# A graph layer on one core: 128 of a bucket's gathered rows are fetched row by row from the SyncE and ScalarE queues

## The reference

```python
h = maximum(layernorm(x), 0)
semb = h[src] @ tokeys.T
oemb = h[src] @ toqueries.T
values = exp(sum(semb * relations[rel] * oemb, axis=1) / 128)
fr = src + n * rel
values = values / segment_sum(values, fr)[fr]
output = segment_sum(values[:, None] * h[dst], fr).reshape(16, n, 128)
weights = einsum('rb,bij->rij', comps, bases_w)
out = x + relu(einsum('rij,rnj->ni', weights, output))
```

## Time and profile before

| | |
|---|---|
| median of 3 runs | 2524.19 us (2522.42 to 2524.29) |
| the profiled execution's own time | 2523.76 us |
| its span, from the first to the last instruction | 2522.1 us |
| POOL busy | 1699.4 us, 67% of the span |
| DVE busy | 1449.6 us, 57% |
| PE busy | 1407.6 us, 56% |
| ACT busy | 506.2 us, 20% |
| DMA engines busy from 510 to 2522 us | 21% |

### The profile page before, as it was taken

The page is one execution under the profiler, slowest core; times in us unless marked ns, Lnnn a source line. Parts: engine busy times, 40 slices in busy tenths (PEclk is TensorE's granted clock), DMA queues, the critical chain, the costliest instruction groups (busy, mean ns, idle before and its releaser), DMA issues.

```text
span 2522.1 us, 30851 instructions
## 1 busy us (share of the span) xinstructions
PE 1407.6 (56%) x9509; PEld 1047.1 (42%) x9510; DVE 1449.6 (57%) x2495; ACT 506.2 (20%) x968; POOL 1699.4 (67%) x1825
## 2 busy tenths in 40 slices
PE   4999999844445454544545364544545364544543
PEld 3666666623424243333424243333434243443423
DVE  7999999965454545445454544445454545445450
ACT  4666666511010101111110101111110101111110
POOL 3333344367777777777777777777777777777775
PEclk9999999966766676766666666766666666766666
DMA  5222222212222222222222222222222222222222
GB/s 156 120 119 115 112 114 119 100 46 55 56 53 56 53 56 53 56 53 56 55 54 55 54 55 54 55 53 56 55 54 55 54 55 54 55 54 55 54 55 41
DMA packets 76390, 169.04 MB, mean 67 GB/s; under 512 B 29162, under 2 KB 43730, under 8 KB 69943
## 3 DMA queue, kind: packets, MB, share of 16 engines
q0 software_dynamic: 52576, 105.77, 16.4%
q1 hardware_dynamic: 23442, 62.88, 6.6%
q10 hardware_dynamic: 352, 0.14, 0.0%
HBM read 112.09 MB, written 56.57 MB: 67 GB/s over the span
## 4 chain that ended last, share of the span: by engine, by line
POOL 58%; issue 20%; PE 17%; DMA 1%; DVE 1%; POOLq 1%; ACT 1%; SPq 0%; DVEq 0%; ACTq 0%
POOL arena L432 58%; PE bank L1055 7%; PE bank L1040 3%; PE bank L1011 1%; PE bank L1013 1%; ACT PFS L875 1%; POOLq L424 1%; DMA bucket_streams<-REC,IDXW 1%; PE bank L1019 1%; PE bank L1016 1%; PE bank L1015 1%; PE bank L1047 1%; DMA stage<-in_edge_type 0%; PE bank L1048 0%; PE bank L1158 0%
## 5 line engine op out<-in xcount | busy, mean ns | idle before, releaser
L432 POOL DMA_INDIRECT arena<-Z_messages,IDX x1593 | 1504.3, 944 | 490.7 <-issue 485.2
L1158 PE MATMUL bank<-arena 128*128 128x128 f32 x3528 | 510.6, 318 | 759.2 <-DMA arena<-Z_messages,IDX 759.2
L1158 PEld LDWEIGHTS bank<-arena 128*128 128x128 f32 x3528 | 502.7, 233 | 769.0 <-issue 769.0
L714 DVE SCALAR_TENSOR_TENSOR O<-bank,X 128x128 f32<-128x128 f32 x49 | 14.3, 292 | 734.1 <-PE bank L1158 734.1
L955 ACT COPY pay_all<-bank 128x1024 bf16<-128x1024 bf16 x147 | 108.0, 807 | 1368.1 <-PE bank L1125 1339.2
L395 POOL DMA_INDIRECT bucket_streams<-REC,IDXW x50 | 87.9, 1758 | 270.8 <-ACT REC L895 135.0
L706 DVE TENSOR_TENSOR arena<-stage,bank 128x512 f32<-128x512 bf16 x441 | 267.9, 682 | 0.3 <-PE bank L1146 0.2
L649 DVE TENSOR_TENSOR stage<-bank,NLF 128x4608 bf16<-128x4608 f32 x49 | 242.4, 4948 | 0.0
L1115 PE MATMUL bank<-stage,OHR 128*128 128x512 bf16 (+1 forms) x441 | 196.4, 611 | 50.7 <-DVE arena L706 44.4
L1146 PE MATMUL bank<-pay_all 128*128 128x256 bf16 x882 | 135.4, 282 | 114.7 <-DVE arena L706 110.0
L1055 PE MATMUL bank<-WT,HT 128*128 128x512 f32 x392 | 183.9, 609 | 0.0
(11 more groups left out here) (168 smaller groups left out, 1819.3 us busy)
## 6 DMA issues: line engine op xcount, KB each, us to landing
Z_messages<-stage SPq DMA_DIRECT2D x48, 1024.0 KB, 3.9
arena<-Z_messages,IDX POOLq DMA_INDIRECT x1593
X<-in_x SPq DMA_DIRECT2D x4, 768.0 KB, 12.8
out<-O SPq DMA_DIRECT2D x48, 64.0 KB
arena<-in_L_gnn_bases_w SPq DMA_DIRECT2D x1, 1024.0 KB, 15.0
bucket_streams<-arena SPq DMA_DIRECT2D x1, 882.0 KB
RL<-bucket_streams SPq DMA_DIRECT2D x49, 18.0 KB
Z_messages<-stage SPq DMA_DIRECT2D x1, 848.0 KB
```

The costliest lines, as they stand in the source:

```text
L432: g.indirect_dma_start(Gbuf[par][:, k, :], None, Z, bass.IndirectOffsetOnAxis(IDX[par][:, k:k + 1], 0))\
L1158: mm = t_.matmul(bank[2][:, 0:EMB], OW[:, k, :], Gbuf[par][:, k, :], start=(k == 0), stop=(k == G - 1))
```

## The change

The first of a bucket's tiles, which POOL gathered, is now fetched row by row. SP fetches its rows 0 to 63 and ACT its rows 64 to 127. Each row is a DMA of its own of 512 bytes. Its row number in `Z` comes from a register, and eight such registers are filled by one load from SBUF. POOL gathers tiles 1 and up. The 36 products of the sum stay.

DVE makes the row numbers of the first tile in one partition (`FIRST`), by a copy and a shift ahead of the `IDX` shift. PE's sum waits for one semaphore more (`row`). The count of POOL's gathers that PE waits for is lower by one in each bucket. SP and ACT wait at the start of the second stage until the table `Z` is stored.

```diff
+def first_tile(b, par):            # on SP; rows 0 to 63
+    sp.wait_ge(s["idx"], b + 1)
+    sp.sem_inc(s["sp_go"], 1)
+    if dyn(b) or b >= 2:
+        sp.wait_ge(s["acc"], b - 1)
+    sp.sem_inc(s["sp_go"], 1)
+    for p in range(0, P // 2, 8):
+        _, rows = nc.values_load_multi_w_load_instructions(
+            FIRST[par][:, 1, p:p + 8], engines=[mybir.EngineType.SP], ...)
+        for k in range(8):
+            sp.dma_start(Gbuf[par][p + k:p + k + 1, 0, :], Z[bass.ds(rows[k], 1), :]).then_inc(row[par], 16)
 def bucket(b, par):                # SP
-    if dyn(b) or b < NB:
-        if dyn(b) or b >= 2:
-            sp.wait_ge(s["rl_t"], b - 1)
-        sp.dma_start(RL[par][:, :], stream[bass.ds(b * (STRIDE // P), G), :]).then_inc(rl[par], 16)
+    if dyn(b) or b + 1 < NB:
+        load_records(b + 1, 1 - par)
+    first_tile(b, par)
     if dyn(b) or b >= 2:
         store_out(b - 2, par)
...
-                    for k in range(FLOOR):           # POOL, gather
+                    for k in range(1, FLOOR):
                         tile(k)
...
                 def gather_index(b, par):          # DVE
+                    v.tensor_copy(FIRST[par][:, 0, :], RL[par][0:1, :]).then_inc(s["first"], 1)
+                    dve.wait_ge(s["first"], b * 2 + 1)
+                    v.tensor_scalar(FIRST[par][:, 1, :], FIRST[par][:, 0, :], 7, None, ALU.logical_shift_right)\
+                        .then_inc(s["first"], 1)
+                    dve.wait_ge(s["first"], b * 2 + 2)
                     v.tensor_scalar(IDX[par][:], RI[:], 7, None, ALU.logical_shift_right).then_inc(s["idx"], 1)
...
                     if dyn(b) or b + 1 < NB:       # ACT, bucket
                         spread_relations(b + 1, 1 - par)
+                    first_tile(b, par)             # as on SP, rows 64 to 127
...
                     pe.wait_ge(gat[par], g_total)  # PE, aggregate
+                    pe.wait_ge(row[par], row_total)
```

More of the change, by code:

```diff
@@ L161, in program @@
         zrow = sb("zrow", [2 * R, EMB], F32)
-        NT = sb("NT", [NB, 6], F32)
+        NT = sb("NT", [NB, 7], F32)
         NTI = sb("NTI", [NB, 2], I32)
@@ L170, in program @@
         IDX = [sb(f"IDX{p}", [P, G], I32) for p in range(2)]
+        FIRST = [sb(f"FIRST{p}", [1, 2, P], I32) for p in range(2)]
         NLI = sb("NLI", [P, 2, G], I32)
@@ L198, in program @@
             h th ht so_mm so_sb prod z_mm z_sb zst0 zst1 zrow v nt nt_mm nt_row marks_sb marks_st
-            rl0 rl1 rl_t ri dec nlf idx inv rrf ohn ohr ord vr cnt cm cx cs masks x3 w w3 bd tp oht lk ow gat0 gat1 acc o ost0 ost1
+            rl0 rl1 rl_t ri dec nlf idx inv rrf ohn ohr ord vr cnt cm cx cs masks x3 w w3 bd tp oht lk ow gat0 gat1 row0 row1 sp_go act_go first acc o ost0 ost1
             pool_go pe_go iota_p
@@ L207, in program @@
         ost = [s["ost0"], s["ost1"]]
+        row = [s["row0"], s["row1"]]
         x_in = [s[f"x_in{k}"] for k in range(5)]
@@ L292, in _, with load_records @@
             with sp.If(bad < 1):
+                def load_records(b, par):
+                    if dyn(b) or b >= 2:
+                        sp.wait_ge(s["rl_t"], b - 1)
+                    sp.dma_start(RL[par][:, :], stream[bass.ds(b * (STRIDE // P), G), :]).then_inc(rl[par], 16)
+                def first_tile(b, par):
+                    sp.wait_ge(s["idx"], b + 1)
+                    sp.sem_inc(s["sp_go"], 1)
+                    if dyn(b) or b >= 2:
+                        sp.wait_ge(s["acc"], b - 1)
+                    sp.sem_inc(s["sp_go"], 1)
+                    for p in range(0, P // 2, 8):
+                        _, rows = nc.values_load_multi_w_load_instructions(
+                            FIRST[par][:, 1, p:p + 8], engines=[mybir.EngineType.SP], min_val=0, max_val=ZROWS - 1,
+                            skip_runtime_bounds_check_because="a record holds a row of Z or the empty row")
+                        for k in range(8):
+                            sp.dma_start(Gbuf[par][p + k:p + k + 1, 0, :], Z[bass.ds(rows[k], 1), :]).then_inc(row[par], 16)
                 def bucket(b, par):
-                    if dyn(b) or b < NB:
-                        if dyn(b) or b >= 2:
-                            sp.wait_ge(s["rl_t"], b - 1)
-                        sp.dma_start(RL[par][:, :], stream[bass.ds(b * (STRIDE // P), G), :]).then_inc(rl[par], 16)
+                    if dyn(b) or b + 1 < NB:
+                        load_records(b + 1, 1 - par)
+                    first_tile(b, par)
                     if dyn(b) or b >= 2:
@@ L305, in store_out @@
                     sp.dma_start(out[bass.ds(b * P, n), :], O[par][0:n, :]).then_inc(ost[par], 16)
+                sp.wait_ge(zst[0], 16 * ((NB + 1) // 2))
+                sp.wait_ge(zst[1], 16 * (NB // 2))
+                load_records(0, 0)
                 bucket(0, 0)
@@ L603, in _ @@
             chain(v.tensor_scalar(NT[:, 1:2], NTI[:, 1:2], float(FLOOR), None, ALU.max), "nt")
+            chain(v.tensor_scalar(NT[:, 6:7], NT[:, 1:2], 1.0, None, ALU.subtract), "nt")
             chain(v.tensor_scalar(PARI[:, 1:2], PARI[:, 0:1], 1, None, ALU.bitwise_and), "nt")
-            chain(v.tensor_tensor(NT[:, 3:4], NT[:, 1:2], PARI[:, 1:2], ALU.mult), "nt")
-            chain(v.tensor_tensor(NT[:, 2:3], NT[:, 1:2], NT[:, 3:4], ALU.subtract), "nt")
+            chain(v.tensor_tensor(NT[:, 3:4], NT[:, 6:7], PARI[:, 1:2], ALU.mult), "nt")
+            chain(v.tensor_tensor(NT[:, 2:3], NT[:, 6:7], NT[:, 3:4], ALU.subtract), "nt")
             chain(v.tensor_scalar(NT[:, 4:5], MX[:], float(WIN), None, ALU.is_gt), "nt")
@@ L958, in bucket, with first_tile @@
                         spread_relations(b + 1, 1 - par)
+                    first_tile(b, par)
+                def first_tile(b, par):
+                    act.wait_ge(s["idx"], b + 1)
+                    act.sem_inc(s["act_go"], 1)
+                    if dyn(b) or b >= 2:
+                        act.wait_ge(s["acc"], b - 1)
+                    act.sem_inc(s["act_go"], 1)
+                    for p in range(P // 2, P, 8):
+                        _, rows = nc.values_load_multi_w_load_instructions(
+                            FIRST[par][:, 1, p:p + 8], engines=[mybir.EngineType.Activation], min_val=0, max_val=ZROWS - 1,
+                            skip_runtime_bounds_check_because="a record holds a row of Z or the empty row")
+                        for k in range(8):
+                            a.dma_start(Gbuf[par][p + k:p + k + 1, 0, :], Z[bass.ds(rows[k], 1), :]).then_inc(row[par], 16)
+                act.wait_ge(zst[0], 16 * ((NB + 1) // 2))
+                act.wait_ge(zst[1], 16 * (NB // 2))
                 spread_relations(0, 0)
@@ L1086, in _ @@
             pe.wait_ge(s["v"], NCH)
-            pe.wait_ge(s["nt"], 10)
+            pe.wait_ge(s["nt"], 11)
             t_.matmul(bank[3][0:1, 0:NB], NT[:, 1:2], identf[0:NB, 0:NB], start=True, stop=True)
@@ L1149, in lookups, with aggregate @@
                         mm.then_inc(s["lk"], 1)
-                def aggregate(b, par):
-                    g_total = pe.value_load(ROWI[0:1, bass.ds(b + (1 + par) * NB, 1)], min_val=16 * FLOOR, max_val=16 * G * (NB + 1) // 2)
+                def aggregate(b, par, row_total):
+                    g_total = pe.value_load(ROWI[0:1, bass.ds(b + (1 + par) * NB, 1)], min_val=16 * FLOOR - 16, max_val=16 * G * (NB + 1) // 2)
                     pe.wait_ge(s["ow"], b * 9 + 9)
                     pe.wait_ge(gat[par], g_total)
+                    pe.wait_ge(row[par], row_total)
                     if dyn(b) or b >= 1:
@@ L1160, in aggregate, with stepb @@
                     mm.then_inc(s["acc"], 1)
-                def stepb(b, par, rl_total):
+                def stepb(b, par, rl_total, row_total=0):
                     if dyn(b) or b + 1 < NB:
@@ L1168, in stepb @@
                     if dyn(b) or b >= 1:
-                        aggregate(b - 1, 1 - par)
+                        aggregate(b - 1, 1 - par, row_total)
                     if dyn(b) or b < NB:
@@ L1174, in _ @@
                 stepb(0, 0, 16)
-                stepb(1, 1, 32)
+                ROWS = 16 * P
+                stepb(1, 1, 32, ROWS)
                 with pe.Fori(1, (NB - 1) // 2) as j:
[L1177 to L1180, removed]
+                    stepb(j * 2, 0, j * 16 + 16, j * ROWS)
+                    stepb(j * 2 + 1, 1, j * 16 + 32, j * ROWS + ROWS)
+                stepb(NB - 1, 0, 0, (NB - 1) // 2 * ROWS)
+                stepb(NB, 1, 0, (NB + 1) // 2 * ROWS)
             with pe.If(bad > 0):
```

## The result

| | before | changed |
|---|---|---|
| median | 2523.61 us (2522.42 to 2524.29, 4 runs) | 2463.59 us (2462.7 to 2464.11, 4 runs) |
| the profiled execution, its span | 2523.76, 2522.1 us | 2462.7, 2461.0 us |

The ratio is 0.9762 with a 95% interval of 0.9745 to 0.9779. The kernel is 60 us faster. The forecast was 2653 us and slower; what happened is its Rival 1 (2463 us): POOL stays the bound.

The account below looks back on a forecast made before the run. The prediction took POOL's gather issue as the present bound and ACT's row fetching, 42.9 us per bucket, as the new one. 533.9 + 49 x 42.9 + 15.4 + 1.7 = 2653 us, 5% slower; range 2458 to 2900 us.

Parts of the forecast that it names:

- Rival 1: Second stage: POOL stays the bound and all row work on SP and ACT is hidden, 2463 us; chance 0.34.
- POOL's part: POOL's gathers: 49 of 1593 go, saving 61.2 us; 39.4 us per bucket, 2462.6 us if POOL remains slowest.
- the price of ACT's bucket: ACT's queue: 64 row transfers, 8 loads and 0.5 us for the rest take 42.9 us per bucket, slowest of all.
- c: Step from one row transfer to the next on a queue: 0.46 us on SP, 0.50 on ACT.
- L: One load of eight registers on SP or ACT: 1.3 us, the middle between 0.3 and 2.3.
- The range: Whole kernel's time: 2458 to 2900 us, leaving out the far end of 3579 us.
- SP's 41.2 us: SP's queue per bucket: 64 x 0.46 + 8 x 1.3 + 1.4 for its two transfers, gaps and loop.
- Rival 2: SP's and ACT's queues hinder one another: c = 0.60, 2967 us; chance 0.12 together with a still dearer load.
- DVE's addition: DVE's copy and shift before IDX: about 0.4 us per bucket, hidden by 13 us of room before POOL.
- The form of the sum: Kernel time: 533.9 before ACT's rows, 49 buckets of ACT, 15.4 to the end, plus 1.7 us.
- the first buckets are in time: PE's sum: first buckets' rows end 63 us after IDX, the sum comes at 70.6 us, so no wait.

Follow-up runs that it names:

- norows: Changed kernel without the row loads, row transfers and PE's wait for them, first tile not fetched: 2463.1 us, ratio 0.9757 to the kernel before.
- scratch: Changed kernel, but POOL gathers all tiles and the fetched rows go to a tile nobody reads: 2524.83 us, ratio 1.0002 to the kernel before.
- sp_all: Changed kernel, but SP fetches all 128 rows of the first tile and ACT none: 3945.63 us, one run.
- rows72_b: Changed kernel with 72 rows on each of SP and ACT, 8 of them into an unread tile: 2536.08 us, ratio 1.0057 to the kernel before.
- rows80_b: Changed kernel with 80 rows on each of SP and ACT, 16 of them into an unread tile: 2726.61 us, ratio 1.0805 to the kernel before.
- load1: Changed kernel with loads of one register instead of eight on SP and ACT: 4180.84 us, one run.

## Why the prediction was wrong

- **POOL's part was right.** 49 x 1.249 = 61.2 us and 2462.6 us for POOL as the bound; 2462.7 was profiled. norows and scratch show the same from both sides.
- **The step that failed is the price of ACT's bucket**, 64 x 0.50 + 8 x 1.3 + 0.5 = 42.9 us, and with it the claim that POOL's 39.4 us are hidden behind ACT. The free buckets without a jump measure 34.2: 64 x 0.42 + 8 x 0.83 = 33.5, and 0.7 for the rest. Of the 8.7 us too many, 5.1 come from c and 3.8 from L; the rest took 0.2 more than forecast. In the forecast's own sum either one alone would have put the bucket below 39.4 (37.8 or 39.1), so it was lost on two prices that both erred upward. The loop's jump, 1.3 us per bucket on average, was no term of it and erred the other way: measured with it, ACT's pace is about 35.3 us.
- **The range** reached down to 2458 us and holds the measured time, but only because it took in Rival 1. The sum of 2653 us and the direction were wrong.
- **L = 1.3** was the middle between "paid once" (0.3) and "each register an access of its own" (2.3). The right picture is a mix: about 0.45 for the load and 0.04 to 0.06 for each register. The Trainium skill's 200 ns per register ("Runtime: NRT & Kernel Launch", Instruction fetch mechanics) would have given 1.6 and does not hold for these loads from SBUF: 0.49, 0.78 and 1.23 us were measured on SP for 1, 8 and 16.
- **c = 0.46 and 0.50** took the shortest known transfer (0.258) as the floor. A one-row transfer is shorter, 0.225, and its arithmetic 0.037 instead of 0.052: 0.05 us together. On ACT I had added 0.04 from two transfers at the kernel's start; ACT's plain row is as cheap as SP's, except behind a load. The lower bound of c was no bound, since no row showed a one-row transfer.
- **SP's 41.2 us** erred the same way: 34.6 measured, 4.1 of the difference from L and 2.6 from c.
- **Rival 2** fell: 228 ns beside ACT, 225 alone (sp_all). The lock of the Trainium skill's "Perfetto Trace Analysis" (DMA Instruction — HWDGE) costs at most 3 ns per transfer in this pattern.
- **DVE's addition** was hidden as forecast (scratch), except once: the first gather starts 0.8 us later. 0.5 us of it is the copy and the shift, which lie between `RI` and `IDX` (0.73 us apart there, 0.23 before).
- **The form of the sum was right.** 533.9 + 49 x bucket + 15.4 gives the spans of rows72_b and rows80_b to about 2 us. And "the first buckets are in time" was wrong: the first three sums waited 27.9 us for rows. This was free, because POOL was then filling the other half of `Gbuf`.

## What to carry to other kernels

Before work is moved to an idle queue, its load per period has to be compared with the bound's; here 35 to 36.5 us against 39.4 gave the whole 60 us, and four microseconds more took it back. When the verdict hangs on two unmeasured prices, it is not one forecast with a range but two outcomes, and neither the middle of a bound nor the shortest known row is evidence: here the middle for L and the floor for c, which was no floor, together chose the wrong one. Where a pace is hidden, look at the start of the stage for buckets that run free, since they show a queue's own pace.

## What was not expected of the hardware

- On ACT the first DMA behind a register load takes 0.454 us where the others take 0.222 (load1; the maximum of 537 in the rows of the changed kernel). On SP there is little of it: load1's `L313` transfers have a median of 255 ns against 225.

```profile
L313 SPq DMA_DIRECT2D arena<-Z_messages x3136: 254/255/283, 514.5 to 4095.5; - x196
```

- A loop with a long body pays for its jump. SP's store and its next record load in the changed kernel, once with the jump between them and once without:

```profile
1506.54 0.39 SPq L325 DMA_DIRECT2D out<-O  x1
...
1510.04 0.31 SPq L299 DMA_DIRECT2D RL<-bucket_streams  x1
...
1547.09 0.39 SPq L325 DMA_DIRECT2D out<-O  x1
1547.69 0.31 SPq L299 DMA_DIRECT2D RL<-bucket_streams  x1
```

The gap is 3.11 us with it and 0.21 without. In the kernel before, with its short body, it is 0.58 with the jump:

```profile
608.16 0.37 SPq L305 DMA_DIRECT2D out<-O  x1
609.11 0.32 SPq L298 DMA_DIRECT2D RL<-bucket_streams  x1
```

So the jump costs about 2.5 us more, 1.3 per bucket, and the queue of instruction fetches (`q14`) carries 268 packets where it carried 10. That it is the length of the body and not the change's new waits is shown by norows, which has the waits but neither loads nor transfers. With the jump:

```profile
608.58 0.38 SPq L319 DMA_DIRECT2D out<-O  x1
609.53 0.33 SPq L299 DMA_DIRECT2D RL<-bucket_streams  x1
```

Its gap is 0.57 us again, and `q14` carries 11 packets. In sp_all SP's body is twice as long and the gap is 3.15 us, so twice the length costs no more. The Trainium skill ("Runtime: NRT & Kernel Launch", Instruction fetch mechanics) says that a taken branch whose target is outside the current two pages waits for a fetch; the traces agree: the wider gap and the many fetch packets are there only with the long bodies. The forecast had no term for it.
